# Second attention: weighted values kept with features in the partitions, softmax sums inverted over memory, a fourth query tile

## The chip, the cores and the metric

The kernel runs on one core of one Trainium2 chip. The metric is the device time of one execution in microseconds. A core has the engines TensorE (PE in the profile; PEld is its weight load), VectorE (DVE), ScalarE (ACT), GpSimd (POOL) and SyncE (SP), which here issues all DMAs. The engines run their own instruction lists and meet at semaphores.

## The reference

Two pre-norm transformer layers in float32, on x of shape (4, 1024, 256):

```
x = x + attn0(layernorm(x))     # 8 heads of 64, low-rank keys and values
x = x + ffn0(layernorm(x))      # 256 -> 1024 -> 1024 -> 1024 -> 256, ternary weights, gated SiLU, two GELUs
x = x + attn1(layernorm(x))     # the second attention: 16 heads of 16, rotary positions
x = x + ffn1(layernorm(x))      # 256 -> 768 -> 256, gated SiLU, weights / 127
```

The second attention, which the change is about:

```
xq, xk, xv = x @ wq.T, x @ wk.T, x @ wv.T      # (4, 1024, 16 heads, 16)
xq, xk = rope(xq), rope(xk)
probs = softmax(einsum('bqhd,bkhd->bhqk', xq, xk) / 4)
out = einsum('bhqk,bkhd->bqhd', probs, xv).reshape(4, 1024, 256) @ wo.T
```

## The kernel before

`attention_a` computes the first attention (0 to about 810 us). `ffn_attention_ffn` does everything behind it with one schedule, written out by hand: a counter H runs from 0 to END, and each engine's program goes through the same H and asks small functions (`x_at`, `norm_at`, `send_at`, ...) what it has to do there. START = 512, LAST = 1024.

H below START is the first FFN: 8 blocks of 512 tokens, 64 slots each, with 22 weight tiles of 512 KB a block that SP loads through three buffers `wt`. Beside a block's matmuls the attention's q, k and v of an earlier block are projected (`PROJECT`, `VALUES`): ScalarE copies the projection to `qk`, GpSimd rotates it to `t1` (`rotate`), ScalarE casts it to the high part `comp[:, 0]` (`send_high`, which waits until the send before has landed), GpSimd computes the low part `comp[:, 1]` (`send_low`), and SP sends both parts to DRAM (`send`). float32 precision is kept in matmuls on fp32r operands by such high and low parts. GpSimd's `low` makes the low parts of the FFN's own activations, for which TensorE waits.

From H = START on comes the second attention, with h = H - START from 0 to 511. A unit u is one batch b, one group g of four heads and one half of 512 queries: 32 units of 16 half steps. In half step h TensorE computes scores(h) (keys in the partitions, two heads side by side), then maxima(h + 24), the scores of half step h + 24 the other way round, and then the weighing, the product of probabilities and values into `psO`. ScalarE takes the exponential of scores(h) (`exponent`), VectorE the maximum over keys of maxima(h + 24) (`reduce`). Scores and maxima take turns on three pairs of PSUM banks (ring `R`): each needs the pair that was used three entries before to be emptied. The negated maxima go back as a row of the query tile (`max_rows`, `keep_rows`, `move_rows`, at step 9 of a unit), so that the exponentials come out shifted. Key tiles `KT` (two) and query tiles `QT` (three) are fetched from DRAM by SP, in six DMAs each (`fetch`).

`psO` holds 4 heads x 17 rows (16 values and the sum of the probabilities, at partitions 32i to 32i + 16) by 512 queries. One half step behind a unit ScalarE copies it to `OS` (`keep_out`, L1600). At step 3 TensorE turns it in four 128x128 transposes into the single bank `psX` (`finish`, L1992), VectorE inverts the sums (L1759) and multiplies (L1765) into `TON`, which has the tokens in the partitions. When a batch is complete, eight tiles of 128 tokens are projected: two transposes turn a tile back (`out_back`, L2000), ScalarE copies it twice (L1636, L1637), GpSimd subtracts (L1870), and two slots later TensorE multiplies it by wo (`project_out`) and VectorE adds the residual (L1786), which SP loads three slots ahead; SP stores the result. These slots are h = 128b + OUT_BACK and OUT = 2 later. All of this shares `psX` in the order of the ring `X`.

From H = LAST on comes the last FFN, 8 blocks of 8 slots. Its first norm is computed during the attention, at D_LOAD, D_STATS and D_SCALE.

Of the kernel before, what the change touches and what calls it, by code (L numbers as in the profile page):

```python
# [1092 lines left out]
def ffn_attention_ffn(nc, x_in, x_mid, x_att, x_out, attn, wcopy, dcopy, c_rope, scratch, shared):  # L1093
# [12 lines left out]

    NB, MT, PER, SLOTS = 8, HID0 // 128, 22, 64
# [10 lines left out]
    QUERY_PARTS, KEY_PARTS = (0, 1, 0), (0, 0, 1)  # L1118
# [7 lines left out]
    OUT_BACK, OUT = (117, 123, 127, 133, 139, 143, 149, 155), 2  # L1126
    D_LOAD, D_STATS, D_SCALE, D_TURN = LAST - 124, LAST - 114, LAST - 112, (LAST - 24, LAST - 20)
# [40 lines left out]

    def x_at(H):
# [61 lines left out]
    def norm_at(H):  # L1231
# [6 lines left out]
        if H in (D_STATS, D_SCALE):  # L1238
            return norm_of["d", 0], int(H == D_SCALE)
# [51 lines left out]
    with ExitStack() as ctx:  # L1291
# [25 lines left out]
        osr = [p.sb(f"osr{i}", [128, 2, 128]) for i in range(2)]  # L1317
# [9 lines left out]
        rinv = p.sb("rinv", [128, 4, NH])  # L1327
        norm.small_tiles(p)

        wd = [comp[:, j // 2, 256 * (j % 2):256 * (j % 2) + 256] for j in range(4)] + [wr["q"][0][:, j, :] for j in range(2)]  # L1330
# [11 lines left out]
        s_K, s_Q = [p.sem(f"K{i}") for i in range(2)], [p.sem(f"Q{i}") for i in range(3)]  # L1342
        s_max, s_rows = p.sem("max"), [p.sem(f"rows{i}") for i in range(3)]
        s_pv, s_os, s_rinv = p.sem("pv"), p.sem("os"), p.sem("rinv")
# [7 lines left out]
        raw = [x[:, :, :].rearrange("p a n -> p (a n)")[:, 0:512].rearrange("p (k n) -> p k n", k=2) for x in P[:3]] + [TON[:, 0:2, :]]  # L1352
# [8 lines left out]
        def sent(kk, what, j):  # L1361

            return s_sent, 16 * (nth[kk, what, j] + 1)

        def key_fetched(gi):
            return s_K[gi % 2], 96 * (gi // 2 + 1)

        def query_fetched(u):
            return s_Q[u % 3], 96 * (u // 3 + 1)
# [4 lines left out]
        def out_index(b, t):  # L1374
            return NT * b + t

# [202 lines left out]
        def scalar(eng):  # L1579
# [599 lines left out]
```

## Time and profile before

| | |
|---|---|
| time, median of 3 runs | 2496.91 us (2495.08 to 2500.58) |
| the profiled execution | 2489.84 us |
| its span | 2488.1 us |
| mean granted TensorE clock | 0.989 of full speed |
| TensorE, VectorE, ScalarE, GpSimd busy in the span | 96%, 60%, 55%, 41% |
| the same over 1900 to 1940 us, inside the second attention | 39.96, 37.33, 31.03 and 0.00 us of 40 |

The profile has for each instruction its start and length in microseconds, and before some the idle time of the engine with the instruction that ended it. Lines L126 and so on are lines of the kernel; L126 is the helper through which nearly all matmuls go, so they are told apart by their tiles: `m_R<-m_Q,m_K` on 64 partitions is a score pair, on 48 partitions a maxima pair, `m_O<-m_P,m_V` is the weighing, `m_X` is what goes through the single bank. A busy TensorE is not TensorE at its peak, since matmuls are pipelined.

### The profile page before, as it was taken

What the parts mean: (1) busy time and instruction counts of PE and PEld (TensorE: products, weight loads), DVE (VectorE), ACT (ScalarE), POOL (GpSimd) and SP (SyncE); (2) the same over time, 40 slices, a digit from 0 to 9 for tenths busy, and PEclk for the clock granted to TensorE, in tenths of its full rate; (3) what the DMA queues carried; (4) which work ended last, traced back from release to release, by engine and by line L of the source; (5) the groups of instructions that cost most, each with busy time, mean ns of one, the idle gap of its engine ahead of it and who ended that gap; (6) DMA issues with size and microseconds to landing.
All of it is one profiled execution on the core that took longest, in us unless ns stands there. A gap on an engine that the chain in (4) does not pass through costs nothing. (4 is left out here: it accounts for less than half of the span.)

```text
span 2488.1 us, 38941 instructions
## 1 busy us (share of the span) xinstructions
PE 2386.9 (96%) x15333; PEld 1471.4 (59%) x15333; DVE 1491.9 (60%) x1965; ACT 1364.9 (55%) x1819; POOL 1008.8 (41%) x656
## 2 busy tenths in 40 slices
PE   6989999999999899999999999999999999999999
PEld 4445555555555688878878877444444444444588
DVE  6676676676774223312222223789889889899364
ACT  3454454454454443443444443477777777777743
POOL 1556675675667346546556556030000000000254
PEclk8999999999999899999999999999999999999999
DMA  2111221211112455555555556423212222321132
GB/s 66 53 66 53 94 69 61 91 59 63 63 52 67 136 169 170 175 188 170 174 187 174 181 174 188 125 69 59 67 44 46 67 44 46 72 48 27 46 100 86
DMA packets 139768, 241.75 MB, mean 97 GB/s; under 512 B 28256, under 2 KB 88544, under 8 KB 139232
## 3 DMA queue, kind: packets, MB, share of 16 engines
q1 hardware_dynamic: 139584, 239.22, 32.1%
q8 instruction: 124, 2.03, 0.4%
q14 instruction: 60, 0.49, 0.1%
HBM read 198.13 MB, written 52.03 MB: 101 GB/s over the span
## 5 line engine op out<-in xcount | busy, mean ns | idle before, releaser
L1736 DVE TENSOR_REDUCE m_mraw<-m_R 128x2 f32<-128x1024 f32 x512 | 625.2, 1224 | 78.2 <-PE m_R L126 72.7
L1594 ACT ACTIVATE m_P<-m_R 128x1024 f32<-128x1024 f32 x512 | 524.5, 1026 | 162.5 <-PE m_R L126 160.0
L581 ACT ACTIVATE a_P<-a_S 128x1024 f32<-128x1024 f32 x256 | 248.9, 1023 | 177.3 <-PE a_S L126 177.2
L126 PE MATMUL m_O<-m_P,m_V 128*17 128x256 f32 x4096 | 329.4, 393 | 2.8 <-ACT m_P L1594 1.1
L1847 POOL TENSOR_TENSOR m_act0l<-m_xf,m_act0h 128x512 fp32r<-128x512 f32 x128 | 164.8, 1290 | 241.6 <-ACT m_xf L1658 137.2
L712 DVE TENSOR_REDUCE a_mraw<-a_X 128x2 f32<-128x1024 f32 x165 | 201.6, 1222 | 101.4 <-PE a_X L126 101.3
L126 PE MATMUL m_R<-m_Q,m_K 64*128 64x512 f32 x1024 | 256.0, 496 | 3.6 <-DVE m_mraw L1736 3.1
L126 PE MATMUL m_R<-m_act0h,wt 128*128 128x512 f32 x640 | 251.4, 393 | 0.0
L126 PE MATMUL m_R<-m_act0l,wt 128*128 128x512 f32 x640 | 250.4, 391 | 0.0
L126 PE MATMUL a_O<-a_P,a_V 128*64 128x512 f32 x1024 | 248.6, 607 | 0.5 <-ACT a_ON L589 0.5
L877 POOL TENSOR_TENSOR a_accp<-a_accp,a_P 128x1024 f32<-128x1024 f32 x96 | 232.5, 2422 | 14.8 <-ACT a_P L581 5.4
L126 PE MATMUL m_R<-m_K,m_Q 48*128 48x512 f32 x1024 | 231.8, 448 | 5.2 <-issue 3.1
L1870 POOL TENSOR_TENSOR m_osp0l<-m_osr,m_osp0h 128x256 fp32r<-128x256 f32 x16 | 11.8, 736 | 551.9 <-ACT m_osr L1637 551.9
L126 PE MATMUL m_R<-m_act1h,wt 128*128 128x512 f32 x512 | 202.9, 396 | 12.5 <-POOL m_act1l L1847 12.5
L126 PE MATMUL m_R<-m_act1l,wt 128*128 128x512 f32 x512 | 203.9, 398 | 0.0
L126 PEld LDWEIGHTS m_R<-m_Q,m_K 64*128 64x128 f32 x1024 | 95.3, 183 | 178.0 <-issue 148.4
L126 PE MATMUL m_R<-next_hi,wt 128*128 128x512 f32 x448 | 178.1, 397 | 12.0 <-issue 10.1
L126 PE MATMUL m_R<-next_lo,wt 128*128 128x512 f32 x448 | 177.2, 396 | 0.0
L126 PEld LDWEIGHTS m_O<-m_P,m_V 128*17 128x17 f32 x4096 | 84.9, 121 | 144.0 <-issue 135.6
L126 PE MATMUL a_X<-a_Kh,a_Qh 64*128 64x512 f32 x496 | 116.9, 464 | 34.2 <-DVE a_mraw L712 18.2
L126 PEld LDWEIGHTS a_X<-a_Kh,a_Qh 64*128 64x128 f32 x496 | 48.9, 184 | 152.7 <-issue 120.1
L126 PEld LDWEIGHTS m_R<-m_K,m_Q 48*128 48x128 f32 x1024 | 96.4, 184 | 68.8 <-ACT m_P L1594 45.8
(236 smaller groups left out, 4258.3 us busy)
## 6 DMA issues: line engine op xcount, KB each, us to landing
wt<-wcopy SPq DMA_DIRECT2D x176, 512.0 KB, 3.4
m_xres<-x SPq DMA_DIRECT2D x96, 128.0 KB, 2.4
m_K<-bounce_k SPq DMA_DIRECT2D x96, 128.0 KB, 4.2
m_Q<-bounce_q SPq DMA_DIRECT2D x192, 64.0 KB, 2.7
m_ln_x<-x SPq DMA_DIRECT2D x23, 512.0 KB, 4.1
a_tile<-in_L_ffn_tiles SPq DMA_DIRECT2D x22, 512.0 KB, 3.7
wcopy<-in_L_ffn_tiles SPq DMA_DIRECT2D x22, 512.0 KB, 5.0
x<-m_xres SPq DMA_DIRECT2D x64, 128.0 KB, 1.8
```

Of the source, the lines that this page charges most:

```text
L126: return pe.eng.matmul(out, lhsT, rhs, start=start, stop=stop, skip_group_check=True)
L581: act.eng.activation(P[n % NP][:, :, :], psS[n % 2][:, :, :], ACT.Exp, scale=SCALE).then_inc(s_exp)
L712: dve.eng.tensor_reduce(mraw[u % 2][:, t, :], psX[:, first:first + 2, :], AX.X, ALU.max).then_inc(X.free(key))
L877: pool.eng.tensor_tensor(accp[:, :, :], accp[:, :, :], P[n % NP][:, :, :], ALU.add).then_inc(s_addp)
L1594: act.eng.activation(P[h % 4][:, :, :], pair(key)[:, :, :], ACT.Exp, scale=SCALE).then_inc(R.free(key))
L1736: dve.eng.tensor_reduce(mraw[u % 2][:, at, :], pair(key)[:, :, :], AX.X, ALU.max).then_inc(R.free(key))
L1847: pool.eng.tensor_tensor(act_buf[dst][1][:, m, :], xf[fs(key) % 2][:, :], f32(act_buf[dst][0][:, m, :]), ALU.subtract).then_inc(s_lo)
L1870: pool.eng.tensor_tensor(osp[t % 2][1][:, :, :], osr[t % 2][:, :, :], f32(osp[t % 2][0][:, :, :]), ALU.subtract).then_inc(s_ol)
```

## The change

The weighted values stay as they come, features in the partitions, queries along the free dimension.

- TensorE: `finish` and `out_back` with their transposes are gone, and so are VectorE's multiply, ScalarE's second copy and the tiles `TON` and `osr`.
- At step 2 behind a unit SP writes `OS` to DRAM (256 KB) and gathers its four rows of sums into `total`, 128 partitions of 16 numbers (`move_sums`). At step 7 VectorE inverts them (`invert`). At step 11 SP writes the inverses to DRAM (`move_inverses`) and fetches the unit's 64 feature rows back into `ON` (`move_heads`, 128 KB). At step 13 SP waits until the inverses have landed and fetches them back spread over 64 partitions (`spread_inverses`, 128 KB) into a half of `yt`, a tile of the first FFN. At step 15 of every second unit GpSimd multiplies 128 partitions x 512 (`normalise`).
- Output tiles are made at h = 128b + SPLIT, four steps apart: ScalarE casts 128 tokens of `ON` to the high part (`out_high`, waits for the multiply), GpSimd subtracts, and 3 slots later TensorE projects. The last batch's eight tiles all fall behind LAST; before, two of them lay ahead of it.
- The scratch of q and k has three parts of 16 rows for each head in place of two shared ones. A send is three DMAs of 256 KB in place of one of 512 KB, and a key or query fetch is two DMAs of 48 rows in place of six of 16 rows with the same bytes.
- `comp` becomes a fourth query tile once the last send has landed: GpSimd clears the rows beside the 48 at START + 46. From unit 6 on queries are fetched 38 half steps ahead of their scores in place of 29; the first six 32 ahead. Keys are fetched two half steps sooner.
- The down weights of the last FFN go to the tiles of wk and wq, in three DMAs in place of two, since `comp` is taken.
- The first norm of the last FFN is loaded at LAST - 90 in place of LAST - 124 and computed in six pieces three steps apart from LAST - 70, in place of two at LAST - 114 and LAST - 112.

```diff
-    OUT_BACK, OUT = (117, 123, 127, 133, 139, 143, 149, 155), 2
-    D_LOAD, D_STATS, D_SCALE, D_TURN = LAST - 124, LAST - 114, LAST - 112, (LAST - 24, LAST - 20)
+    SPLIT, OUT = (128, 132, 136, 140, 144, 148, 152, 156), 3
+    SUMS, INVERT, INVERSES, SPREAD, NORMALISE = 2, 7, 11, 13, 15
+    QUERY_TILES = [0, 1, 2, 0, 1] + [(3, 2, 0, 1)[(u - 5) % 4] for u in range(5, NU)]
+    D_LOAD, D_PIECES, D_TURN = LAST - 90, [LAST - 70 + 3 * i for i in range(6)], (LAST - 24, LAST - 20)
...
+    def split_at(H):
+
+        for b in range(B):
+            if H - START - 128 * b in SPLIT:
+                return b, SPLIT.index(H - START - 128 * b)
+        return None
+
+    def ended_unit_at(H, slot):
+
+        u, hh = divmod(H - START, 16)
+        return u - 1 if hh == slot and 0 <= u - 1 < NU else None
...
-        if hh == 3 and 0 <= u - 1 < NU:
-            return "finish", u - 1
         if hh == 9 and 0 <= u + 1 < NU:
             return "rows", u + 1
-        for name, o in (("out_back", h), ("out", h - OUT)):
-            for b in range(B):
-                if o - 128 * b in OUT_BACK:
-                    return name, b, OUT_BACK.index(o - 128 * b)
+        if split_at(H - OUT):
+            return "out", *split_at(H - OUT)
...
+        tiles_filled = KT + QT
+        QT = QT + [comp]
         mrow = [p.sb(f"mrow{i}", [16, 128], F32R) for i in range(2)]
         OS = p.sb("OS", [128, 512])
-        TON = p.sb("TON", [128, NT, 256])
...
+        ON = p.sb("ON", [128, 2, T])
...
-                dst = scratch[what][b][:, 128 * j:128 * j + 128, 512 * half:512 * half + 512].rearrange("s p n -> p s n")
-                sp.eng.dma_start(dst, f32(comp[:, :, :])).then_inc(s_sent, 16)
+                dst = scratch[what][b][8 * j:8 * j + 8, :, :, 512 * half:512 * half + 512]
+                for s, part in enumerate((0, 1, 0) if what == "q" else (0, 0, 1)):
+                    sp.eng.dma_start(dst[:, s, :, :], f32(comp[:, part, :])).then_inc(s_sent, 16)
...
-                for i, part in enumerate(src):
-                    heads = part.rearrange("(i h r) n -> h r i n", i=2, h=2)
-                    for h in range(2):
-                        rows = slice(64 * h + 16 * i, 64 * h + 16 * i + 16)
-                        sp.eng.dma_start(f32(tile[rows, :, :]), heads[h]).then_inc(sem, 16)
+                heads = src.rearrange("(i h) s r n -> h (s r) i n", h=2)
+                for h in range(2):
+                    sp.eng.dma_start(f32(tile[64 * h:64 * h + 48, :, :]), heads[h]).then_inc(sem, 16)
...
+            def move_sums(u):
+
+                sp.wait_ge(s_os, u + 1)
+                if u >= 2:
+                    sp.wait_ge(s_heads[u % 2], 16 * (u // 2))
+                sp.eng.dma_start(scratch["os"][u % 2], OS[:, :]).then_inc(s_bounce, 16)
+                sp.wait_ge(s_rinv, u)
+                sp.eng.dma_start(total[:, :], OS[16:128:32, :]).then_inc(s_total, 16)
+
+            def move_heads(u):
+
+                (first, f, cols), (b, g, half) = heads_of(u), unit(u)
+                if b:
+                    sp.wait_ge(s_ol, out_index(b - 1, 4 * half + 4))
+                sp.wait_ge(s_norm[half], (NG * b + g) // 2)
+                sp.wait_ge(s_bounce, 16 * (u + 1))
+                heads = scratch["os"][u % 2].rearrange("(i r) n -> i r n", i=NH)[:, 0:16, :]
+                sp.eng.dma_start(ON[first:first + 64, f, cols], heads).then_inc(s_heads[half], 16)
+
+            def move_inverses(u):
+                sp.wait_ge(s_rinv, u + 1)
+                if u >= 2:
+                    sp.wait_ge(s_spread[u % 2], 16 * (u // 2))
+                sp.eng.dma_start(scratch["inv"][u % 2].rearrange("h (p c) -> (h p) c", c=16), rinv[:, :]).then_inc(s_rout, 16)
+
+            def spread_inverses(u):
+
+                (first, _, _), (b, g, half) = heads_of(u), unit(u)
+                sp.wait_ge(s_rout, 16 * (u + 1))
+                sp.wait_ge(s_norm[half], (NG * b + g) // 2)
+                if u < 2:
+                    sp.wait_ge(*X.filled(("back", NB - 1, 3)))
+                wide = scratch["inv"][u % 2].rearrange("h (o n) -> h o n", o=1).to_broadcast([NH, 16, 512])
+                sp.eng.dma_start(yt[half][first:first + 64, :], wide).then_inc(s_spread[half], 16)
...
-                gi, u = (h + 30) // 32, (h + 29) // 16
-                if (h + 30) % 32 == 0 and 0 <= gi < B * NG:
+                gi, u = (h + 32) // 32, (h + 38) // 16
+                if (h + 32) % 32 == 0 and 0 <= gi < B * NG:
                     fetch_key(gi)
-                if (h + 29) % 16 == 0 and 0 <= u < NU:
+                if (h + 32) % 16 == 0 and 0 <= (h + 32) // 16 < 6:
+                    fetch_query((h + 32) // 16)
+                if (h + 38) % 16 == 0 and 6 <= u < NU:
                     fetch_query(u)
+                if ended_unit_at(H, SUMS) is not None:
+                    move_sums(ended_unit_at(H, SUMS))
+                if ended_unit_at(H, INVERSES) is not None:
+                    move_inverses(ended_unit_at(H, INVERSES))
+                    move_heads(ended_unit_at(H, INVERSES))
+                if ended_unit_at(H, SPREAD) is not None:
+                    spread_inverses(ended_unit_at(H, SPREAD))
...
-                    act.wait_ge(*X.filled(("finish", u - 1)))
+                    act.wait_ge(s_total, 16 * u)
+                    act.wait_ge(s_bounce, 16 * u)
...
-            def keep_back(b, t):
-                i, key = out_index(b, t), ("out_back", b, t)
-                src = psX[0][:, 0:256].rearrange("p (f n) -> p f n", f=2)
-                act.wait_ge(*X.filled(key))
+            def out_high(b, t):
+                i = out_index(b, t)
+                act.wait_ge(s_norm[t // 4], 2 * b + 2)
                 if i >= 2:
                     act.wait_ge(*X.filled(("out", *divmod(i - 2, NT))))
-                    act.wait_ge(s_ol, i - 1)
-                act.eng.activation(osp[t % 2][0][:, :, :], src, ACT.Copy).then_inc(s_oh)
-                act.eng.activation(osr[t % 2][:, :, :], src, ACT.Copy).then_inc(X.free(key))
+                act.eng.activation(osp[t % 2][0][:, :, :], ON[:, :, 128 * t:128 * t + 128], ACT.Copy).then_inc(s_oh)
...
-            def finish(u):
-                b, g, half = unit(u)
-                key = ("finish", u)
-                view = psX[0][:, :].rearrange("p (q h c) -> p q h c", q=4, h=NH)
-                dve.wait_ge(*X.filled(key))
-                if u:
-                    dve.wait_ge(*X.emptied(("finish", u - 1)))
-                dve.eng.reciprocal(rinv[:, :, :], view[:, :, :, 16]).then_inc(s_rinv)
-                dve.wait_ge(s_rinv, u + 1)
-                if b:
-                    dve.wait_ge(*X.filled(("out_back", b - 1, 4 * half + 3)))
-                out = TON[:, 4 * half:4 * half + 4, 64 * g:64 * g + 64].rearrange("p q (h d) -> p q h d", h=NH)
-                wide = rinv[:, :, :].rearrange("p q (h o) -> p q h o", o=1).to_broadcast([128, 4, NH, 16])
-                dve.eng.tensor_tensor(out, view[:, :, :, 0:16], wide, ALU.mult).then_inc(X.free(key))
+            def invert(u):
+                dve.wait_ge(s_total, 16 * (u + 1))
+                dve.wait_ge(s_rout, 16 * u)
+                dve.eng.reciprocal(rinv[:, :], total[:, :]).then_inc(s_rinv)
...
+            def normalise(b, f, half):
+
+                cols = slice(512 * half, 512 * half + 512)
+                pool.wait_ge(s_heads[half], 16 * (NG * b + 2 * f + 2))
+                pool.wait_ge(s_spread[half], 16 * (NG * b + 2 * f + 2))
+                pool.eng.tensor_tensor(ON[:, f, cols], ON[:, f, cols], yt[half][:, :], ALU.mult).then_inc(s_norm[half])
+
             def out_low(b, t):
-                pool.wait_ge(*X.emptied(("out_back", b, t)))
-                if out_index(b, t) >= 2:
-                    pool.wait_ge(*X.filled(("out", *divmod(out_index(b, t) - 2, NT))))
-                pool.eng.tensor_tensor(osp[t % 2][1][:, :, :], osr[t % 2][:, :, :], f32(osp[t % 2][0][:, :, :]), ALU.subtract).then_inc(s_ol)
+                i = out_index(b, t)
+                pool.wait_ge(s_oh, i + 1)
+                if i >= 2:
+                    pool.wait_ge(*X.filled(("out", *divmod(i - 2, NT))))
+                pool.eng.tensor_tensor(osp[t % 2][1][:, :, :], ON[:, :, 128 * t:128 * t + 128], f32(osp[t % 2][0][:, :, :]), ALU.subtract).then_inc(s_ol)
...
+            def fill_queries():
+
+                pool.wait_ge(s_sent, 48 * len(nth))
+                for h in range(2):
+                    pool.eng.memset(f32(comp[64 * h + 32:64 * h + 64, :, :]), 0.0).then_inc(s_qfill)
...
-            def finish(key):
-                pe.wait_free(X, key)
-                pe.wait_ge(s_os, key[1] + 1)
-                for q in range(4):
-                    ins = pe.eng.transpose(psX[0][:, 128 * q:128 * q + 128], OS[:, 128 * q:128 * q + 128], ident[:, :])
-                ins.then_inc(X.full(key))
...
-            def out_back(key):
-                _, b, t = key
-                pe.wait_free(X, key)
-                pe.wait_ge(*X.emptied(("finish", UB * b + 6 + t // 4)))
-                for f in range(2):
-                    ins = pe.eng.transpose(psX[0][:, 128 * f:128 * f + 128], TON[:, t, 128 * f:128 * f + 128], ident[:, :])
-                ins.then_inc(X.full(key))
...
-    scratch = {n: [nc.dram_tensor(f"bounce_{n}{i}", [2, 256, T], F32, kind="Internal").ap() for i in range(B)] for n in "qk"}
+    scratch = {n: [nc.dram_tensor(f"bounce_{n}{i}", [16, 3, 16, T], F32, kind="Internal").ap() for i in range(B)] for n in "qk"}
...
+    scratch["os"] = [nc.dram_tensor(f"bounce_os{i}", [128, 512], F32, kind="Internal").ap() for i in range(2)]
+    scratch["inv"] = [nc.dram_tensor(f"inverses{i}", [4, 512], F32, kind="Internal").ap() for i in range(2)]
```

The rest of the diff renames semaphore counts to fit (a send counts 48, a fetch 32), replaces QT[u % 3] by QT[QUERY_TILES[u]], and lets `wd` point to the new tiles.

## Rows read from the trace of the kernel before

**Rows 1.** The page's line of busy times

```profile
PE 2386.9 (96%) x15333; PEld 1471.4 (59%) x15333; DVE 1491.9 (60%) x1965; ACT 1364.9 (55%) x1819; POOL 1008.8 (41%) x656
```

**Rows 2.** Timeline, 1892 to 1896: start us, us, engine, line, operation, tiles, [idle before, releaser]

```profile
1892.68 1.03 ACT L1594 ACTIVATE m_P<-m_R 128x1024 f32<-128x1024 f32 x1 [0.37 <-PE m_R L126]
...
1893.76 0.49 PE L126 MATMUL m_R<-m_K,m_Q 48*128 48x512 f32 x2
...
1894.18 0.65 PE L126 MATMUL m_O<-m_P,m_V 128*17 128x256 f32 x8
1894.30 2.47 DVE L1736 TENSOR_REDUCE m_mraw<-m_R 128x2 f32<-128x1024 f32 x2 [0.16 <-PE m_R L126]
...
1894.76 0.50 PE L126 MATMUL m_R<-m_Q,m_K 64*128 64x512 f32 x2
...
1895.30 1.02 ACT L1594 ACTIVATE m_P<-m_R 128x1024 f32<-128x1024 f32 x1 [0.36 <-PE m_R L126]
```

**Rows 3.** Timeline of ScalarE: four of the 32 copies that end a unit

```profile
1755.06 0.60 ACT L1600 ACTIVATE m_OS<-m_O 128x512 f32<-128x512 f32 x1
...
1832.04 0.60 ACT L1600 ACTIVATE m_OS<-m_O 128x512 f32<-128x512 f32 x1
...
1897.52 0.60 ACT L1600 ACTIVATE m_OS<-m_O 128x512 f32<-128x512 f32 x1
...
1919.35 0.60 ACT L1600 ACTIVATE m_OS<-m_O 128x512 f32<-128x512 f32 x1
```

**Rows 4.** Timeline, the finish of one unit

```profile
1900.10 0.66 PE L1992 MATMUL m_X<-ident,m_OS 128*128 128x128 f32 x4
...
1900.69 0.50 PE L126 MATMUL m_R<-m_Q,m_K 64*128 64x512 f32 x2
...
1900.79 0.26 DVE L1759 RECIPROCAL m_rinv<-m_X 128x16 f32<-128x16 f32 x1
...
1901.09 0.42 DVE L1765 TENSOR_TENSOR m_TON<-m_X,m_rinv 128x256 f32<-128x256 f32 x1
```

**Rows 5.** Timeline, one output tile turned back and copied

```profile
1770.28 0.44 PE L2000 MATMUL m_X<-ident,m_TON 128*128 128x128 f32 x2
...
1770.64 0.50 PE L126 MATMUL m_R<-m_Q,m_K 64*128 64x512 f32 x2
...
1771.03 0.38 ACT L1637 ACTIVATE m_osr<-m_X 128x256 f32<-128x256 f32 x1
```

**Rows 6.** Timeline of VectorE: the two longest waits for a residual in the attention

```profile
1978.88 0.42 DVE L1786 TENSOR_TENSOR m_xres<-m_X,m_xres 128x256 f32<-128x256 f32 x1 [1.89 <-DMA m_xres<-x]
...
2167.32 0.42 DVE L1786 TENSOR_TENSOR m_xres<-m_X,m_xres 128x256 f32<-128x256 f32 x1 [3.36 <-DMA m_xres<-x]
```

**Rows 7.** The page's DMA issues: out<-in, xcount, KB each, us to landing

```profile
a_rinv<-sums SPq DMA_DIRECT2D x62, 128.0 KB, 2.9
...
sums<-a_rcol SPq DMA_DIRECT2D x31, 4.0 KB, 1.4
```

**Rows 8.** Timeline of one block of the first FFN, around the sends

```profile
1045.68 0.37 SPq L1481 DMA_DIRECT2D bounce_k<-m_comp  x1
...
1050.80 0.63 ACT L1613 ACTIVATE m_comp<-m_t 128x512 fp32r<-128x512 f32 x1 [1.12 <-POOL m_t L1859]
...
1052.97 1.28 POOL L1864 TENSOR_TENSOR m_comp<-m_t,m_comp 128x512 fp32r<-128x512 f32 x1
...
1059.67 0.50 PE L126 MATMUL m_R<-m_act1h,wt 128*128 128x512 f32 x1 [1.93 <-POOL m_act1l L1847]
```

**Rows 9.** Timeline, first units of the attention: a send and the next cast

```profile
1643.10 0.42 SPq L1481 DMA_DIRECT2D bounce_q<-m_comp  x1
...
1649.28 0.63 ACT L1613 ACTIVATE m_comp<-m_t 128x512 fp32r<-128x512 f32 x1
```

**Rows 10.** The tile comp, 900 to 1560 us: landing of its sends

```profile
DMA to landing us min/median/max: 2.8/4.2/6.5
```

**Rows 11.** Windows, first FFN: busy us by engine (instructions), clock, DMA share, GB/s

```profile
1020.00:1060.00 40.00, 38.07 (x179) 31.31 (x178) 13.90 (x34) 17.09 (x28) 27.35 (x23) 1.00 0.53 180
```

More of the change, by code:

```diff
@@ L1361, in sent, with query_use, query_freed, rows_moved @@
         def sent(kk, what, j):
-            return s_sent, 16 * (nth[kk, what, j] + 1)
+            return s_sent, 48 * (nth[kk, what, j] + 1)
         def key_fetched(gi):
-            return s_K[gi % 2], 96 * (gi // 2 + 1)
+            return s_K[gi % 2], 32 * (gi // 2 + 1)
+        def query_use(u):
+            return QUERY_TILES[:u + 1].count(QUERY_TILES[u])
+        def query_freed(u):
+            before = [v for v in range(u) if QUERY_TILES[v] == QUERY_TILES[u]]
+            return R.filled(("scores", 16 * before[-1] + 15)) if before else None
+        def rows_moved(u):
+            return s_rows[QUERY_TILES[u]], 32 * query_use(u)
         def query_fetched(u):
-            return s_Q[u % 3], 96 * (u // 3 + 1)
+            return s_Q[QUERY_TILES[u]], 32 * query_use(u)
         def values_fetched(b, t):
@@ L1375, in out_index, with heads_of @@
             return NT * b + t
+        def heads_of(u):
+            b, g, half = unit(u)
+            return 64 * (g % 2), g // 2, slice(512 * half, 512 * half + 512)
         def tile_of_tokens(ap, x):
@@ L1518, in fetch_query @@
                 sp.wait_ge(*sent(2 * b + half, "q", g // 2))
-                if u >= 3:
-                    sp.wait_ge(*R.filled(("scores", 16 * (u - 2) - 1)))
+                if query_freed(u):
+                    sp.wait_ge(*query_freed(u))
+                elif QUERY_TILES[u] == 3:
+                    sp.wait_ge(s_qfill, 2)
                 cols = slice(512 * half, 512 * half + 512)
-                fetch(QT[u % 3], [scratch["q"][b][i, 64 * g:64 * g + 64, cols] for i in QUERY_PARTS], s_Q[u % 3])
+                fetch(QT[QUERY_TILES[u]], scratch["q"][b][4 * g:4 * g + 4, :, :, cols], s_Q[QUERY_TILES[u]])
@@ L1729, in norm_step, with norm_piece @@
                     norm.scale(dve, i, 0, 4)
+            def norm_piece(i, piece):
+                if piece < 2:
+                    norm.stats(dve, i, 2 * piece, 2 * piece + 2)
+                    if piece == 1:
+                        norm.eps(dve, i)
+                else:
+                    norm.scale(dve, i, piece - 2, piece - 1)
             def reduce(k):
@@ L1882, in gpsimd @@
                     send_low(*send_high_at(H)[1:])
-                if x_of(H, "out_back"):
-                    out_low(*x_at(H)[1:])
+                if split_at(H):
+                    out_low(*split_at(H))
+                if ended_unit_at(H, NORMALISE) is not None:
+                    b, g, half = unit(ended_unit_at(H, NORMALISE))
+                    if g % 2:
+                        normalise(b, g // 2, half)
                 if x_of(H, "project"):
@@ L1954, in maxima @@
                     rows = slice(64 * h, 64 * h + 48)
[L1955 removed]
+                    ins = mm(pe, pair(key)[:, h, :], QT[QUERY_TILES[u]][rows, i, 128 * q:128 * q + 128], KT[u // 2 % 2][rows, i, 512 * kh:512 * kh + 512])
                 ins.then_inc(R.full(key))
@@ L1969, in scores @@
                     rows = slice(64 * j, 64 * j + 64)
-                    ins = mm(pe, pair(key)[:, j, :], KT[u // 2 % 2][rows, i, 128 * t:128 * t + 128], QT[u % 3][rows, i, :])
+                    ins = mm(pe, pair(key)[:, j, :], KT[u // 2 % 2][rows, i, 128 * t:128 * t + 128], QT[QUERY_TILES[u]][rows, i, :])
                 ins.then_inc(R.full(key))
```

61 lines of the change are left out of this document (30 added, 31 removed).

## The prediction

> **What bounds the kernel now.** I began with the page: TensorE counts as busy for 96% of the span, VectorE for 60% [rows 1]. A busy TensorE says little, since its matmuls are pipelined, so for the second attention (from about 1570 to 2336 us; only here does the change touch steady work) I read the timeline step by step.
>
> A half step is one score pair on TensorE, one exponential on ScalarE, one maxima pair on TensorE, one reduction on VectorE and one weighing on TensorE. Three pairs of banks serve scores and maxima in turn, so a maxima pair needs the bank that the exponential of the half step before empties. Follow [rows 2]: the exponential from 1892.68 ends at 1893.71; the maxima start at 1893.76, the weighing at 1894.18, the next score pair at 1894.76, its exponential at 1895.30. That closes the ring: 2.62 us for two half steps, 1.31 each, and nothing in it waits for VectorE. VectorE does two reductions in 2.47 us and then idles 0.16. So the ring TensorE-ScalarE binds, and VectorE follows 0.16 us per two steps behind being the bound itself. That is the point on which the forecast turns: work taken from TensorE's queue shortens the ring, work added to VectorE is free only while it is small.
>
> A unit of 16 half steps without an output tile takes 1919.35 - 1897.52 = 21.83 us [rows 3]; 16 x 1.31 is 21.0, so 0.8 us goes to the turning of the sums, the row of maxima and the copy of psO. The three units in which eight output tiles are made take 1832.04 - 1755.06 = 76.98 us [rows 3], 11.5 more than three plain ones: 1.43 us for each tile.
>
> **Finish of a unit (32 times).** Removed: four transposes on TensorE, a reciprocal and a multiply on VectorE. The transposes start at 1900.10 where the score pair would, and that pair starts at 1900.69 [rows 4]: 0.59 us in the ring, 32 x 0.59 = 18.9 us. On VectorE 0.26 + 0.42 = 0.68 us goes. Added there: a reciprocal of as many elements from SBUF, in the half step that also has the small reduction of the maxima. No row has its exact form; it is between 0 and 0.26 us [rows 4] and meets 0.16 us of idle time per two steps. I take 0.06 us on the ring (nearly all fits), 1.9 us in all; bounds 0 and 8.3.
>
> The copy of psO stays on ScalarE. Its new wait, for the gather and the bounce of the unit before, was met some 12 half steps ago. Five new DMAs per unit go through SP; the query fetch shrinks from six issues to two, and SP was mostly waiting.
>
> **Output tiles (32).** Removed: two transposes (1770.28 to the score pair at 1770.64: 0.36 us of ring [rows 5]) and one of two copies of 0.38 us on ScalarE [rows 5]. ScalarE's gaps in the ring are 0.2 to 0.4 us, so the second copy costs between 0 and 0.38; I take 0.10, since the whole tile costs 1.43 and the six projection matmuls and the residual, which stay, need most of it. In the first three batches 24 x 0.46 = 11.0 us; the last batch's eight now all fall behind the attention, where TensorE is filled anyway: 8 x 0.36 = 2.9 us. Together 13.9, bounds 11.5 and 24. GpSimd's subtraction stays and hides.
>
> **Late residuals.** In each batch one residual add sits on VectorE until its load lands; the worst two idles are 1.89 and 3.36 us [rows 6]. Each comes right after SP issued a key fetch and a query fetch of six DMAs each. With two DMAs each, the query at another half step and the norm load moved away, SP reaches the load some 5 us sooner. Units with these waits are about 0.8 and 2.4 us longer than the first batch's, so I give back 3.0 us (bounds 0 and 4).
>
> **Norm of the last FFN.** The same 3.3 us of VectorE work, in six pieces, moves from a stretch where VectorE had gaps round the output tiles to one without. Over 18 half steps the idle 0.16 per two takes 1.4 of it: +1.5 us, after I let the banks' slack take 0.4 (bounds 0 and 3.3).
>
> **The round trip of the sums.** psO is copied at half step 1, inversion stands at 7, sending at 11, spreading at 13, GpSimd's multiply at 15, and at 16 ScalarE waits for it before the first output tile, with the exponentials queued behind. From the gather to the inversion there are about 5 x 1.31 = 6.6 us; small transfers of the first attention's sums land in 1.4 us [rows 7], a broadcast of 128 KB in 2.9 us [rows 7]: 3 us to spare even with 256 KB ahead. From step 11 to 16 there are again 6.6 us, and needed are 1.4 + 2.9 + 1.3 (multiply, the length of a 128x512 subtraction on GpSimd [rows 8]) = 5.6. One microsecond spare, less what SP's rows and query issues take. This matters twice a batch; with output tiles in between, the second has room. I put 0.5 us on three places: +1.5 (bounds 0 and 12).
>
> **Sending q and k.** One DMA of 512 KB becomes three of 256 KB, a duplicate part more: 1.5 times the bytes. ScalarE's next cast waits for them. In the FFN a send is issued at 1045.68, the next cast runs at 1050.80, GpSimd takes it up at 1052.97 [rows 8], so it may slip 1.5 us. GpSimd's low part releases TensorE, which already idles 1.93 us per block [rows 8]; each microsecond beyond the slip would lengthen that. In the first units the gap is 1649.28 - 1643.10 = 6.2 us [rows 9], with exponentials behind. The best landing of a send is 2.8 us [rows 10]. The share of 0.53 at 180 GB/s [rows 11] means 21 GB/s per DMA engine, 1.6 us of data and 1.2 fixed; with half as much again on 16 engines 3.5 us, all hidden. If the new pattern, whose outer dimension counts 8 heads, used only eight engines: 96 KB each, 4.7 + 1.2 = 5.9 us, still inside 6.2, and 0.8 late in the FFN, inside the 1.5. For the third send of a block, already waited for, I add 0.25 us to each of eight blocks: +2 (bounds 0 and 16).
>
> The Trainium skill ("DMA: Bandwidth & Descriptors", section "Why a DMA increments its semaphore by 16 and not by 1") says the number of engines is the largest up to 16 that divides the slowest dimension of both sides. By it the sends run on eight and the broadcast, four heads against 64 partitions, on four; the forecast would stay, the rivals of late transfers would gain. No transfer of before has such a shape, so no row here shows it.
>
> **The fourth query tile.** It is the send buffer, cleared by GpSimd once the last send has landed, first fetched at step 48 and used at 56: ten microseconds. Once +0.5 us (bounds 0 and 3). Later fetches come 11 half steps after the tile is free; before they showed no wait of TensorE, so fetching sooner gains nothing by itself.
>
> **Sum.** -18.9 + 1.9 - 13.9 - 3.0 + 1.5 + 1.5 + 2 + 0.5 = -28.4 us. The profiled execution took 2489.84 us (span 2488.1): 2461.4. The median shown is 2496.91, 7.1 us above it; carried over, 2468.5.
>
> **Rivals.**
> 1. VectorE binds instead. It idles only 0.16 us in 2.62; if the ring tightens, the unit gains only what VectorE loses: 0.68 - 0.26 = 0.42 x 32 = 13.4 us, nothing for the output tiles, 3.0 for the residuals, and the costs of 5.5 stay: -10.9, 2486. For it: the reductions alone are 19.6 us of a unit. Against it: its idle time falls behind TensorE's maxima in the ring.
> 2. The sends land late. If ScalarE waits 2 us more at three places in the first units and the FFN's idle time grows by 1 us or more per block, +14: 2482. For it: the ready margin of 1.5 us; against it: the landing worked out above.
> 3. ScalarE waits at the first output tiles, 1.5 us at eight places, 12 in place of 1.5: 2479.
> 4. Slower: the gather of four rows into 128 partitions of 64 bytes lands after VectorE's step 7, and VectorE, with the reductions behind the waiting reciprocal, stops in every unit. Break-even is 28.4 / 32 = 0.9 us a unit, that is a landing near 7.5 us; at 9 us it would cost 2.4 a unit, 77 in all less 28: 2545. Against it: the 1.4 us.
> 5. Two of 1 to 3 together bring it near no change, 2495.
>
> **Chances.** Forecast 0.62, rival 1 0.13, rival 2 0.09, rival 3 0.07, rival 5 0.04, rival 4 0.05. A measurement of this kernel can tell about 0.2% (5 us) from no change. Faster is the forecast and rivals 1 to 3, 0.91; same 0.04; slower 0.05. The likeliest case with its bounds spans 2459 to 2478: all transposes and copies on the ring at the low end, the reciprocal and the norm pieces uncovered at the high end. To hold rivals 1 to 3 the range reaches to 2486.
>
> **What would show it.** Units without output tiles at 21.3 us (21.8 now); with rival 1 they stay above 21.4 and VectorE shows no idle time ahead of its reductions. An output tile at 0.95 us in place of 1.43. No residual add waiting for a DMA in the attention. VectorE's reciprocal near 0.2 us without idle ahead of it; if there is, rival 4. ScalarE's idle ahead of its cast of ON at the first tile of a batch: under 1 us, else rival 3. TensorE's idle per FFN block 1.9 to 2.2 us, else rival 2. The prediction fails if the FFN span before 1570 us grows by more than 5 us, or if a plain unit stays at 21.8.

## The result and the profile after

The changed kernel takes 2547.31 us (median of 4 runs, 2546.12 to 2549.71), the kernel before 2498.11 in the runs beside it: a ratio of 1.0199 (1.0181 to 1.0216), 49 us slower. The forecast was 2468.5, faster. The profiled execution took 2546.51 us, with a span of 2544.7 us at a mean granted clock of 0.976 (before 0.989).

The page after: busy times (against [rows 1]), the chain that ended last, and the sends of k among the DMA issues.

```profile
PE 2384.2 (94%) x15141; PEld 1467.5 (58%) x15141; DVE 1475.6 (58%) x1933; ACT 1351.5 (53%) x1787; POOL 1031.5 (41%) x674
...
PE 49%; DMA 9%; POOL 3%; ACT 2%; SPq 2%; issue 1%; DVE 1%; ACTq 0%; POOLq 0%; DVEq 0%
...
bounce_k<-m_comp SPq DMA_DIRECT2D x48, 256.0 KB
```

Transfers hold 9% of the chain. The copies of psO on ScalarE tell where the time went. After, in the timeline of ScalarE:

```profile
1678.30 0.60 ACT L1674 ACTIVATE m_OS<-m_O 128x512 f32<-128x512 f32 x1
1707.96 0.59 ACT L1674 ACTIVATE m_OS<-m_O 128x512 f32<-128x512 f32 x1
1740.48 0.60 ACT L1674 ACTIVATE m_OS<-m_O 128x512 f32<-128x512 f32 x1
...
1825.42 0.60 ACT L1674 ACTIVATE m_OS<-m_O 128x512 f32<-128x512 f32 x1
...
1901.75 0.60 ACT L1674 ACTIVATE m_OS<-m_O 128x512 f32<-128x512 f32 x1
1923.01 0.60 ACT L1674 ACTIVATE m_OS<-m_O 128x512 f32<-128x512 f32 x1
1944.27 0.60 ACT L1674 ACTIVATE m_OS<-m_O 128x512 f32<-128x512 f32 x1
```

The first unit's copy stands at 1678.30, before at 1610.45: 67.9 us are lost ahead of it, in the first FFN and the first slots of the attention. From the first copy to the last (2394.90) it is 716.6 us against 727.65, so the attention gained 11 us. The tail behind is the same (149.8 and 150.0 us). A plain unit takes 1944.27 - 1923.01 = 21.26 us (21.24 in most; 21.83 in [rows 3]). Three units with eight output tiles take 1901.75 - 1825.42 = 76.33 against 76.98 [rows 3], and the first two steps between copies 29.66 and 32.52 against 30.05 and 27.24.

**The loss in the FFN.** The waits after, 900 to 1640 us: us in total, times, longest.

```profile
ACT m_comp L1687 <- DMA bounce_k<-m_comp: 57.3, 14, 4.8
...
ACT m_comp L1687 <- DMA bounce_q<-m_comp: 45.6, 7, 8.7
...
PE m_R L126 <- DMA wt<-wcopy: 34.3, 7, 6.1
...
PE m_R L126 <- POOL m_act1l L1919: 18.2, 7, 2.6
...
PE m_X L126 <- DVE m_t L1830: 7.7, 9, 1.2
```

Before, TensorE waited in the FFN for GpSimd, 12.5 us in 7, and not for weights, and ScalarE waited for a send of q alone, 22.5 us in 7. One block after, in the timeline of all engines (SPq are SyncE's DMA issues):

```profile
1056.84 1.91 SPq L1510 DMA_DIRECT2D bounce_k<-m_comp  x3
...
1065.42 0.63 ACT L1687 ACTIVATE m_comp<-m_t 128x512 fp32r<-128x512 f32 x1 [4.58 <-DMA bounce_k<-m_comp]
...
1066.13 1.26 POOL L1936 TENSOR_TENSOR m_comp<-m_t,m_comp 128x512 fp32r<-128x512 f32 x1 [1.98 <-ACT m_comp L1687]
...
1067.42 1.90 SPq L1510 DMA_DIRECT2D bounce_q<-m_comp  x3
...
1074.95 0.63 ACT L1687 ACTIVATE m_comp<-m_t 128x512 fp32r<-128x512 f32 x1 [6.19 <-DMA bounce_q<-m_comp]
...
1076.99 1.88 SPq L1510 DMA_DIRECT2D bounce_k<-m_comp  x3
...
1085.51 0.63 ACT L1687 ACTIVATE m_comp<-m_t 128x512 fp32r<-128x512 f32 x1 [3.49 <-DMA bounce_k<-m_comp]
...
1086.21 1.29 POOL L1936 TENSOR_TENSOR m_comp<-m_t,m_comp 128x512 fp32r<-128x512 f32 x1 [2.77 <-ACT m_comp L1687]
...
1087.53 1.88 SPq L1510 DMA_DIRECT2D bounce_q<-m_comp  x3
1089.45 1.36 SPq L1463 DMA_DIRECT2D wt<-wcopy  x1
...
1097.12 0.76 PE L126 MATMUL m_R<-m_act1h,wt 128*128 128x512 f32 x1 [5.04 <-DMA wt<-wcopy]
```

Read it as a chain: a landing, a cast, a low part, the next send. A send is issued at 1056.84 and ScalarE can write the buffer again at 1065.42, 8.6 us later. GpSimd's low part follows that cast, the next send follows GpSimd, and so the four sends of a block stand one behind another; the second, third and fourth cast wait. SyncE works through its queue in order: it waits for GpSimd ahead of the send of 1087.53, and the weight load queued behind that send goes out at 1089.45 only. The load is slow too: TensorE goes on with it at 1097.12, 7.7 us after its issue, where the page's median landing of these loads is 3.4 us. TensorE stops for it 5.04 us. Then it is slow itself. Windows, after (the first one in the attention) and in the last line one block before: busy us of PE, PEld, DVE, ACT and POOL with the number of instructions, granted clock, DMA share, GB/s:

```profile
1850.00:1853.00 3.00, 2.85 (x18) 1.04 (x22) 1.32 (x2) 1.94 (x4) 0.00 (x0) 0.61 0.64 174
1097.00:1100.00 3.00, 2.88 (x9) 2.42 (x10) 0.00 (x0) 0.37 (x1) 0.00 (x0) 0.50 0.62 252
1100.00:1103.00 3.00, 3.00 (x9) 2.32 (x8) 0.69 (x1) 0.22 (x1) 0.00 (x0) 0.50 0.01 4
...
1079.00:1081.00 2.00, 2.00 (x13) 1.75 (x12) 0.00 (x0) 0.64 (x2) 1.92 (x3) 1.00 0.49 160
...
992.72:1097.12 104.40, 95.74 (x424) 78.13 (x425) 29.44 (x57) 41.97 (x68) 53.03 (x42) 0.96 0.55 173
...
1059.67:1154.82 95.15, 93.20 (x424) 76.70 (x424) 24.36 (x50) 42.43 (x69) 53.16 (x42) 0.98 0.53 177
```

From 1097 to 1103 TensorE, busy without a gap, is granted 0.50, the lower of its two levels, 1.2 in place of 2.4 GHz; what came ahead is the idle stretch of 5 us. Six microseconds at half the clock are 3 us of work lost. In other blocks it is less (0.53 and 0.91 in the two windows of 3 us behind the stop that ends at 1202.57, 1.7 us lost). The sum closes: the same stop returns every 104.3 us (992.72 to 1514.40, five blocks), where a block before takes 95.1 us (1059.67 in [rows 8], the next at 1154.82). With as many matmuls TensorE is busy for 95.2 us of a block after (mean of the five) and for 93.2 before: 2.0 of the 9.2 us are matmuls that ran slower, the price of the clock. The other 7.2 are idle time: 5.6 for the weights, 0.7 more for GpSimd's low part, and 0.9 for the values' projection behind VectorE.

**The loss in the attention.** The end of a trip of the sums after, in the timeline:

```profile
1836.41 1.40 SPq L1558 DMA_DIRECT2D m_Q<-m_mrow  x2
1837.87 0.90 SPq L1531 DMA_DIRECT2D m_Q<-bounce_q  x2
...
1839.34 0.38 SPq L1583 DMA_DIRECT2D inverses<-m_rinv  x1
...
1842.60 0.57 SPq L1593 DMA_DIRECT2D m_yt<-inverses  x1
...
1847.39 1.26 POOL L1943 TENSOR_TENSOR m_ON<-m_ON,m_yt 128x512 f32<-128x512 f32 x1 [63.44 <-DMA m_yt<-inverses]
1848.69 0.42 ACT L1708 ACTIVATE m_osp0h<-m_ON 128x256 fp32r<-128x256 f32 x1 [3.24 <-POOL m_ON L1943]
```

Issuing the inverses' send to GpSimd's start is 8.05 us: 3.3 until the spread can be issued, 4.8 until it has landed, where I had put 1.4 + 2.9. A fetch of queries, two DMAs of 192 KB, went out just ahead. It is so in every unit: in the attention after, the sends of the inverses landed in 3.3 us in the median. ScalarE stands 3.24 us here, at the first tiles of the next two batches 4.96 and 2.64 us, once 0.63 us at a second half, and 2.63 us in the last batch, behind the attention. The row of windows for 1850 to 1853 above shows what comes behind: the clock at 0.61.

### The profile page after: what moved, and what is told of

Same layout as the page of the kernel before. It is cut to its first block, busy times and chain, and to the rows that moved or that the text cites. A ratio compares the mean times of both kernels' runs of the same rounds, so it can differ in the third digit from the quotient of the medians.

```text
span 2544.7 us, 38661 instructions
## 1 busy us (share of the span) xinstructions
PE 2384.2 (94%) x15141; PEld 1467.5 (58%) x15141; DVE 1475.6 (58%) x1933; ACT 1351.5 (53%) x1787; POOL 1031.5 (41%) x674
## 4 chain that ended last, share of the span: by engine, by line
PE 49%; DMA 9%; POOL 3%; ACT 2%; SPq 2%; issue 1%; DVE 1%; ACTq 0%; POOLq 0%; DVEq 0%
PE m_R L126 36%; PE m_O L126 10%; DMA bounce_k<-m_comp 4%; DMA wt<-wcopy 2%; PE m_X L126 2%; DMA bounce_q<-m_comp 2%; SPq L1510 2%; POOL m_comp L1936 1%; ACT m_P L1667 1%; DMA m_yt<-inverses 1%; ACT m_comp L1687 1%; DMA inverses<-m_rinv 1%; PE m_X L219 1%; ACT m_OS L1674 0%; DVE m_mraw L1816 0%
## 5 line engine op out<-in xcount | busy, mean ns | idle before, releaser
L126 PE MATMUL m_R<-m_act1h,wt 128*128 128x512 f32 x512 | 210.5, 411 | 52.5 <-DMA wt<-wcopy 34.3
L126 PE MATMUL m_R<-m_act1l,wt 128*128 128x512 f32 x512 | 209.5, 409 | 0.0
L1943 POOL TENSOR_TENSOR m_ON<-m_ON,m_yt 128x512 f32<-128x512 f32 x16 | 20.5, 1279 | 456.2 <-DMA m_yt<-inverses 456.2
L126 PE MATMUL m_R<-m_Q,m_K 64*128 64x512 f32 x800 | 202.3, 502 | 3.0 <-DVE m_mraw L1816 2.8
L126 PE MATMUL m_R<-m_K,m_Q 48*128 48x512 f32 x800 | 183.9, 455 | 4.0 <-ACT m_P L1667 3.9
L126 PEld LDWEIGHTS m_R<-m_Q,m_K 64*128 64x128 f32 x800 | 75.2, 185 | 154.0 <-issue 126.0
L126 PEld LDWEIGHTS m_R<-m_act1h,wt 128*128 128x128 f32 x512 | 101.4, 198 | 79.8 <-issue 39.0
```

The costliest lines, as they stand in the source:

```text
L126: return pe.eng.matmul(out, lhsT, rhs, start=start, stop=stop, skip_group_check=True)
L1943: pool.eng.tensor_tensor(ON[:, f, cols], ON[:, f, cols], yt[half][:, :], ALU.mult).then_inc(s_norm[half])
```

## The experiments

Eight kernels ran, in two groups of four; the kernel before had a median of 2494.48 us beside the first group and 2498.14 beside the second (13 runs each), so ratios are compared.

**e1, the changed kernel with the old sends.** The old scratch, one send of 512 KB, and six DMAs for a fetch:

```diff
-    for s, part in enumerate((0, 1, 0) if what == "q" else (0, 0, 1)):
-        sp.eng.dma_start(dst[:, s, :, :], f32(comp[:, part, :])).then_inc(s_sent, 16)
+    sp.eng.dma_start(dst, f32(comp[:, :, :])).then_inc(s_sent, 16)
```

> The changed kernel with the sends, the scratch and the fetches of q and k as before: one send of 512 KB, six DMAs a fetch; all the rest of the change stays. Theory A (the first FFN loses its 50 us and the first units 5 us because each send, in three DMAs whose outer dimension counts 8 heads, runs on eight DMA engines and lands after 8.5 us in place of 5, so ScalarE's next cast, GpSimd's low part, SP's next send and the weight load queued behind it are late): unit 0 ends near 1610 us again, and the time is 56 + 5 us less than that of the changed kernel, 0.995 of before (2485). Theory B (the five DMAs per unit and the later norm already disturb, and the FFN's loss lies elsewhere, for instance in the tiles' new places): stays above before, over 2520.

Measured: 2499.56 us, 1.0015 (1.0004 to 1.0026), 15 us above the 2485 expected. The first copy of psO is back at 1617.97, and the FFN's waits for weights are gone (0.3 us), as expected. But ScalarE waits longer at the first output tiles (26 us in six waits in the attention, where the changed kernel has 11 in four). The timeline of e1:

```profile
1773.25 3.07 SPq L1532 DMA_DIRECT2D m_Q<-bounce_q  x6
...
1776.88 0.38 SPq L1584 DMA_DIRECT2D inverses<-m_rinv  x1
...
1786.75 0.42 ACT L1709 ACTIVATE m_osp0h<-m_ON 128x256 fp32r<-128x256 f32 x1 [5.89 <-POOL m_ON L1944]
```

The six issues of a fetch stand ahead of the trip: the inverses leave 5.1 us behind the issue of the rows, against 2.9 in the changed kernel. They land sooner (the spread goes out 1.75 us later, at 1778.63, against 3.3), but the spread releases GpSimd only after 6.8 us, against 4.8, with the six DMAs of a key fetch issued behind it. The sends explain the FFN; the fetches that came with them had been worth something in the attention, which I had not expected to see so large.

**e2, the kernel before with the new sends alone** (the same edit the other way round, with scratch and fetches).

> The kernel before with only the sends, the scratch and the fetches of q and k as changed. Theory A: about +60 us, 2555 to 2560, with unit 0 ending near 1678 us; six issues less per two fetches give back the residuals' late loads, 3 us. Theory B: within 10 us of before.

Measured: 2562.25 us, 1.0275 (1.0250 to 1.0300), 2 us above the range expected. The first copy is at 1676.34, plain units stay at 21.83 us. TensorE's largest wait, 900 to 1560 us:

```profile
PE m_R L126 <- DMA wt<-wcopy: 30.5, 6, 6.3
```

Nothing else of the change is in this kernel, and its first fetch goes out at 1579.0, behind the blocks counted here. So the sends alone cause the FFN's loss.

**e3, three sends with another order of the scratch.** The same three DMAs of 256 KB and two per fetch, but rows ahead of parts, so that the outer dimension of a send counts 128 rows, not 8 heads (the three dots leave out the indices):

```diff
-    dst = scratch[what][b][8 * j:8 * j + 8, :, :, 512 * half:512 * half + 512]
+    dst = scratch[...][8 * j:8 * j + 8, ...].rearrange("a r s n -> (a r) s n")
-    heads = src.rearrange("(i h) s r n -> h (s r) i n", h=2)
+    heads = src.rearrange("(i h) r s n -> h (r s) i n", h=2)
-    scratch = ... nc.dram_tensor(f"bounce_{n}{i}", [16, 3, 16, T], ...)
+    scratch = ... nc.dram_tensor(f"bounce_{n}{i}", [16, 16, 3, T], ...)
```

> The changed kernel with the three parts inside each row of the scratch (16 heads, 16 rows, 3 parts, 1024) in place of outside the rows: the same three sends of 256 KB and the same two DMAs a fetch, the same bytes, but the outer dimension of a send now counts 128 rows. Theory A (number of DMA engines): a send lands in about 4.5 us, ScalarE waits for it little, the FFN's loss is gone to within 5 us, time near 2480 to 2487. Rival (the bytes, 1.5 times as many, or three issues of 0.6 us on SP's queue): the FFN keeps most of its loss, time over 2520.

Measured: 2479.56 us, 0.9924 (0.9897 to 0.9950): with the bytes and the number of DMAs unchanged 64 us are gone by the medians, each taken against the kernel before beside it, and 69 by the ratios. TensorE no longer waits for weights; its wait for GpSimd in the FFN of e3, the timeline round the second send of a block, and a window over the first:

```profile
PE m_R L126 <- POOL m_act1l L1919: 12.3, 7, 1.9
```

```profile
1053.37 0.63 ACT L1687 ACTIVATE m_comp<-m_t 128x512 fp32r<-128x512 f32 x1 [1.10 <-POOL m_t L1931]
...
1056.85 1.39 SPq L1510 DMA_DIRECT2D bounce_q<-m_comp  x3
...
1062.49 0.63 ACT L1687 ACTIVATE m_comp<-m_t 128x512 fp32r<-128x512 f32 x1 [3.59 <-DMA bounce_q<-m_comp]
```

```profile
1049.00:1051.00 2.00, 2.00 (x13) 1.73 (x12) 1.97 (x6) 0.28 (x1) 2.00 (x3) 1.00 0.98 367
```

So neither the third part nor the number of issues costs anything that counts in the FFN; the order of the dimensions does. The k send of 1048.25 is no longer waited for by the cast of 1053.37, 5.1 us on, where after it took 8.6; the q send takes 1062.49 - 1056.85 = 5.6 us where after it took 7.5. The windows agree: soon after a k send went out the 16 DMA engines are busy at a share of 0.98 with 367 GB/s in e3, and of 0.49 with 160 GB/s after (1079 to 1081). The fetches read as many rows of the same length as before this edit, and their median landings are the same within 0.4 us (3.3 and 6.1 us for queries and keys; 3.5 and 6.4 in the changed kernel), so it is the sends that changed. A profile of e3 has the first copy at 1618.82, one of e4, the same up to there, at 1611.38: so much do single profiles differ.

**e4, e3 with the trip of the inverses two slots earlier.**

```diff
-    SUMS, INVERT, INVERSES, SPREAD, NORMALISE = 2, 7, 11, 13, 15
+    SUMS, INVERT, INVERSES, SPREAD, NORMALISE = 2, 7, 9, 11, 13
```

> As the run with the parts inside the rows, and the inverses sent at step 9, spread at 11 and the multiply at 13 in place of 11, 13 and 15. Theory C (ScalarE's waits of 3.2, 5.0 and 2.6 us at the first output tile of each batch are the late end of the sums' round trip, which stands behind the row of maxima and the query fetch in SP's queue): these waits fall below 0.5 us and the time by 9 to 15 us against the run without it (each wait also halves TensorE's clock for a while). Rival (the trip is limited by the data's own landing): they shrink by less than half.

Measured: 2463.51 us, 0.9874 (0.9856 to 0.9893), 16 us less than e3 by the medians, 12.5 by the ratios. The timeline of e4, the same place as above for after:

```profile
1761.50 0.32 SPq L1583 DMA_DIRECT2D inverses<-m_rinv  x1
...
1763.53 1.38 SPq L1558 DMA_DIRECT2D m_Q<-m_mrow  x2
1764.95 0.91 SPq L1531 DMA_DIRECT2D m_Q<-bounce_q  x2
...
1766.38 0.58 SPq L1593 DMA_DIRECT2D m_yt<-inverses  x1
...
1773.03 0.42 ACT L1708 ACTIVATE m_osp0h<-m_ON 128x256 fp32r<-128x256 f32 x1 [0.47 <-POOL m_ON L1943]
```

The inverses now leave ahead of the rows and the queries. ScalarE's waits, 11.3 us in e3 (2.49, 0.21, 4.00, 2.53, 0.37, 1.72), are 0.47 and 0.38. The three units with output tiles take 71.4, 71.1 and 71.4 us: 1823.98 - 1752.54 = 71.44 between the copies of the first batch, against 76.98 [rows 3]. From the first copy of psO to the last it takes 694.38 us, in e3 709.36: 15.0 less. 7.9 of them are idle time of TensorE; the other 7.1 are busy time, 685.80 against 692.85 us with the same 6143 matmuls, at a granted clock of 1.00 against 0.99. So nearly half of what the waits cost came behind them, in slow stretches as the window of 1850 shows one for after. The inverses now land in 1.8 us in the median, in e3 3.1.

**e5, e4 with two DMAs for a send** (high and low part as one, the repeated part as the other).

> The run with rows in the scratch and the early trip, and each send in two DMAs (both parts of the send buffer in one of 512 KB, the repeated part in another of 256 KB) in place of three of 256 KB. Theory A: with 16 engines the sends no longer bind, so nothing changes beyond 0.2%. Rival (the count of DMAs still costs on SP's queue): 3 us or more faster.

Measured: 2462.49 us, 0.9847 (0.9822 to 0.9873), the interval overlapping that of e4. The number of issues for a send is not worth anything once it lands in time.

**e6, e4 with three query tiles and the fetch times of before** (and without GpSimd's clearing of a fourth).

```diff
-    QUERY_TILES = [0, 1, 2, 0, 1] + [(3, 2, 0, 1)[(u - 5) % 4] for u in range(5, NU)]
+    QUERY_TILES = [u % 3 for u in range(NU)]
-    gi, u = (h + 32) // 32, (h + 38) // 16
+    gi, u = (h + 30) // 32, (h + 29) // 16
```

> The run with rows in the scratch and the early trip, but with three query tiles as before, fetched 29 half steps ahead (keys 30), and nothing cleared by GpSimd. Theory: the fourth tile and the earlier fetch are worth nothing by themselves, since a fetch of two DMAs lands in time either way: within 0.2%. Rival: the fetches again fall before the residual loads of the output tiles and behind the sums' trip: VectorE waits for residuals 1 us or more in each batch, and the time rises by 3 to 8 us.

Measured: 2459.21 us, 0.9839 (0.9816 to 0.9863), the same as e5 beside it. The fourth tile and the sooner fetch bring nothing; with fetches outside the slots of the trip ScalarE does not wait at a first tile at all.

**e7, the changed kernel with two send buffers in turn.** The sends keep the pattern by heads; the second buffer is half of ON, idle until the attention's first gather:

```diff
+    comps = [comp, ON[:, 1, :].rearrange("p (a n) -> p a n", a=2).bitcast(F32R)]
-    act.wait_ge(s_sent, 48 * i)
-    act.eng.activation(comp[:, 0, :], t1[:, :], ACT.Copy).then_inc(s_chi)
+    if i >= 2:
+        act.wait_ge(s_sent[i % 2], 48 * (i // 2))
+    act.eng.activation(comps[i % 2][:, 0, :], t1[:, :], ACT.Copy).then_inc(s_chi)
```

> The changed kernel as it is, sends on eight engines included, but casts and sends alternate between two send buffers (the second is the half of ON that is free until then), so ScalarE waits for the send before the last. Theory A1 (the FFN's loss is a chain: send lands late, ScalarE's cast, GpSimd's low part, then SP stands in its queue at the next send and issues the weight load behind it 5 us late): with the waits of ScalarE gone the FFN loses at most 10 of the 56 us, time near 2490 to 2500. Rival A2 (eight of sixteen engines are filled with the sends, and the weights' data behind them are late by themselves): TensorE still waits for weights, time over 2520.

Measured: 2495.21 us, 0.9989 (0.9975 to 1.0003). The pattern of the transfers is that of the changed kernel, but ScalarE waits for no landing. Its waits, 900 to 1560 us, and one of these stops with the load that ends it:

```profile
ACT m_comp L1691 <- POOL m_t L1935: 20.5, 14, 2.0
PE m_R L126 <- DMA wt<-wcopy: 15.1, 7, 2.6
```

```profile
1171.37 1.89 SPq L1513 DMA_DIRECT2D bounce_q<-m_ON  x3
1173.31 1.30 SPq L1465 DMA_DIRECT2D wt<-wcopy  x1
...
1181.03 0.47 PE L126 MATMUL m_R<-m_act1h,wt 128*128 128x512 f32 x1 [2.31 <-DMA wt<-wcopy]
```

The first copy of psO is at 1627.11, 51 us sooner than after. That is the chain shown from the other end: with the same transfers, freeing ScalarE of the landing brings back three quarters of the loss. A block takes 97.6 us (986.69 to 1474.60, five blocks), so 2.5 of the 9.2 us remain, 17 in seven blocks, more than the 10 that I had allowed for. Here rival A2 has a part. The load is not issued late any more: counted from the matmul that GpSimd's low part releases in the same block, it goes out after 12.4 us (1173.31 less 1160.89), in e3 after 13.4 and in the changed kernel after 16.7. But it releases TensorE 7.7 us after its issue, as in the changed kernel, where in e3 TensorE does not stop for it. So what is left is a load that is slow beside sends of this pattern.

**e8, e4 with two send buffers.**

> The run with rows in the scratch and the early trip, with two send buffers as well. What still waits for a send there is ScalarE once a block, 3 to 5 us, and TensorE's idle time of 1.9 us per block is released by GpSimd's low part. Theory: GpSimd's own queue of rotations sets that idle time, not the send: within 0.2% of the run without it. Rival: the wait for the send holds GpSimd back, and 1 to 2 us per block, 8 to 15 us, are gained.

Measured: 2459.35 us, 0.9841 (0.9817 to 0.9864), as e5 and e6. With sends over all the engines the second buffer is not needed.

## Why the prediction was wrong

**The step that failed: sending q and k, +2 us (bounds 0 and 16).** It measured 64 to 69 us by e3 (the medians, and 1.0199 less 0.9924, of 2498) and 68 by e2 alone (2562.25 less 2494.48). Four things were wrong in it, one behind another.

The landing: I computed 5.9 us for eight engines as if the three DMAs began together. They are issued one after another in 1.9 us by SyncE, and 8.6 us go by before the buffer is free. With 1.9 us of issuing the 5.9 become 7.8, near what the rows show, and beyond the 6.2 us that I had read as the room in the first units.

The slip: "0.8 late in the FFN, inside the 1.5" compared one send with one gap. But each send waits for the cast and the low part that follow the send before, so lateness adds up over the four sends of a block: the casts in the rows after waited 4.58, 6.19 and 3.49 us. e3 shows the buffer ready for three of four casts, and a wait only where there was one before.

The queue: I priced the wait at ScalarE and GpSimd, and never asked what stands behind the next send in SyncE's queue. It is the FFN's own weight load, which has nothing to do with the attention. TensorE waited 34.3 us for it in all. And beside a send the load itself needed 7.7 us, which was not in the sum either; e7 shows that this part is about a quarter. My rival 2 had the right place and +14; it lacked the same step.

The clock: each stop of 5 us was followed by a stretch at 1.2 GHz, 2.0 us more per block in the mean. Nothing in the sum stood for that.

The rule that I had set beside this term gives eight engines for an outer dimension of 8, and sixteen for the 128 rows of e3 (the Trainium skill, "DMA: Bandwidth & Descriptors", section "Why a DMA increments its semaphore by 16 and not by 1"). The two windows agree with it: half the share of the DMA engines at 160 GB/s against nearly all at 367; a share is a mean over the engines, so it does not name the ones that worked. I had written that no transfer of before has such a shape; the rows of maxima leave eight partitions, but with 4 KB they show no rate. I had the 5.9 us, and put the price of the chain behind it at nothing.

**The second step: the round trip, +1.5 us (bounds 0 and 12).** It measured 12.5 to 16 us (e4 against e3), beyond the bound of 12 and of rival 3's kind. Two causes: the rows and the query fetch stand ahead of the inverses in SyncE's queue, though I wrote "less what SP's rows and query issues take" and then took nothing; and the landings with a fetch under way were 3.3 and 4.8 us, not the 1.4 and 2.9 of the first attention [rows 7]. Rival 3 counted 12 us at eight places; there were six in e3, three of them above 2 us, and the clock on top. Both steps together are 73 to 81 us more than the sum had for them, and that is the whole miss: from the forecast of 28.4 us less to the measured 49.2 us more it is 78.

**The first units.** The same sends cost 4.9 us there (29.66 + 32.52 against 57.29), where rival 2 had put 2 us at three places. In e3 they take 29.68 and 26.57.

**What was right.** The finish: 21.83 to 21.24 us, 0.59 a unit as read from [rows 4], and the reciprocal cost nothing. After, in VectorE's timeline:

```profile
1931.63 0.19 DVE L1823 TENSOR_REDUCE m_mneg<-m_mraw 128x16 fp32r<-128x32 f32 x1
1931.74 0.24 DVE L1835 RECIPROCAL m_rinv<-m_total 128x16 f32<-128x16 f32 x1
...
1938.42 2.47 DVE L1816 TENSOR_REDUCE m_mraw<-m_R 128x2 f32<-128x1024 f32 x2 [0.17 <-PE m_R L126]
```

It has no idle time ahead (in the attention one reciprocal waits for its gather, 7.55 us in the last unit, where one waited 7.64 before too), so the gather is in time. Rival 4 had named the time 2545 that came out, but its mechanism is not what happened: its number was luck. The sign that I had set for a failure did appear: the stretch ahead of the attention grew by 67.9 us, where 5 were allowed. And VectorE's idle time is still 0.17 us in two steps, so rival 1 is out too: the ring shrank and VectorE with it. An output tile costs 0.9 us (a unit with four of them, undisturbed, 24.86 less 21.24), against 0.95. No residual waits for its load in the attention after. The pieces of the norm cost 0.87 us in place of 1.5.

**The sum that would have held.** Where both disturbances are taken out (e4), the kernel is 1.3% faster than before (31 us), and 1.5 to 1.6% in e5, e6 and e8 (38 to 40 us, one less their ratios, times 2498). The forecast of -28.4 is then a little short. In the profiles the attention of e4 is 33.3 us shorter than before (694.38 against 727.65), where the terms that fall in it make 27.5. The reciprocal that cost nothing and the cheaper norm are 2.5 of the difference. I cannot name the rest: the spread of before between the two groups alone is 3.7 us.

## What to carry to other kernels

Before a transfer's pattern is changed, follow its landing round the whole loop: who waits for the buffer, what that engine then releases, which send comes next, and what unrelated load stands behind that send in the same queue; lateness adds up over every turn of such a loop. Write the outer dimension of a DMA so that it counts many rows: here the order of two scratch dimensions alone made 64 to 69 us. And price a short round trip over memory by landings read beside the fetches that will be under way with it, and give it the slot ahead of them.

## What the runs showed of the hardware

Three things that I had not expected. Three DMAs of 256 KB kept the 16 DMA engines at a share of 0.98 or 0.49, and were issued in 1.39 or 1.90 us, by nothing but the order of the dimensions in memory (128 rows or 8 heads outside). A small transfer is slower right behind a large one: the same inverses landed in 3.3 us in the median where two DMAs of 192 KB had gone out just ahead (after; 3.1 in e3), and in 1.8 where none had (e4, e6). In e1, behind six DMAs of 64 KB, it was 1.8 too, so the bytes ahead are not all that counts. And a stop of TensorE is dearer than its length: behind 5 us of idle time, 6 us followed with a granted clock of 0.50, though TensorE was busy throughout; behind ScalarE's wait of 3.24 us in the attention it was 0.61 over 3 us.
